# Other states of a selective scan take their forcing term through a diagonal matrix

## The reference, cut to what matters

```python
dt = softplus(proj[..., :512] + dt_bias)            # (T=256, 512 channels)
Bm, Cm = proj[..., 512:576], proj[..., 576:]        # (T, 64 states) each
A = -exp(A_log)
def step(hst, ins):
    dt_t, B_t, C_t, x_t = ins
    dA = exp(dt_t[:, :, None] * A)
    hst = hst * dA + (dt_t * x_t)[:, :, None] * B_t[:, None, :]
    y_t = einsum('bds,bs->bd', hst, C_t)
    return (hst, y_t)
```

## Time and profile before

| | |
|---|---|
| median of 3 runs | 3304.09 us (3300.77 to 3307.41) |
| the profiled execution | 3316.36 us, its span 3314.5 us |
| granted TensorE clock, mean | 0.97 of full speed |
| busy share of PE, PEld, DVE, ACT, POOL | 92%, 83%, 87%, 88%, 88% |
| the seventh pass (forward), 1350 to 1547 us | PE 189.7, DVE 181.9, ACT 180.7, POOL 181.4 us busy |
| the eighth pass (backward), 1547 to 1740 us | PE 180.2, DVE 176.5, ACT 181.2, POOL 182.6 us busy |

### The profile page before, as it was taken

How to read it: one execution, slowest core, us unless ns; L and a number is a source line. 1 busy time by engine, 2 the same in 40 slices (tenths; PEclk the granted TensorE clock), 3 DMA queues, 4 the chain that set the end, 5 groups by cost and what they waited for, 6 DMA issues and landing times.

```text
span 3314.5 us, 71769 instructions
## 1 busy us (share of the span) xinstructions
PE 3058.3 (92%) x23032; PEld 2760.6 (83%) x23032; DVE 2884.0 (87%) x3203; ACT 2904.8 (88%) x6357; POOL 2911.3 (88%) x1552
## 2 busy tenths in 40 slices
PE   8778999999999999999999999999999999998877
PEld 6568988898888988889888898888888898887766
DVE  2269999899989998899998999899988999989985
ACT  1189999898989989899998999899898989989993
POOL 0069999998999999999998999999999999999995
PEclk6699999999999999999999999999999999999998
DMA  5011111111111111111111111112111111111210
GB/s 179 0 42 45 45 46 54 43 52 44 46 51 45 52 44 47 51 50 44 46 54 44 51 45 45 53 45 52 44 47 50 51 46 45 45 50 44 55 47 26
DMA packets 163039, 162.61 MB, mean 49 GB/s; under 512 B 17610, under 2 KB 156874, under 8 KB 162644
## 3 DMA queue, kind: packets, MB, share of 16 engines
q1 hardware_dynamic: 162644, 157.69, 17.5%
HBM read 154.44 MB, written 3.18 MB: 48 GB/s over the span
## 4 chain that ended last, share of the span: by engine, by line
PE 50%; ACT 23%; issue 11%; DVE 8%; POOL 7%; DVEq 0%; ACTq 0%; POOLq 0%; DMA 0%; SPq 0%
PE ps L1263 13%; ACT dA L584 12%; PE ps L1247 12%; ACT uBT L570 6%; PE ps L1010 6%; POOL hst L417 5%; DVE hst L909 5%; PE ps L1245 4%; PE ps L1082 3%; PE ps L1019 3%; PE ps L1057 3%; PE ps L1066 1%; PE ps L1255 1%; PE ps L1131 1%; POOL uBT L430 1%
## 5 line engine op out<-in xcount | busy, mean ns | idle before, releaser
L417 POOL TENSOR_TENSOR hst<-hst,C_sb 128x1024 f32<-128x1024 f32 x1024 | 2447.3, 2407 | 176.1 <-DVE hst L909 172.7
L909 DVE TENSOR_TENSOR_SCAN hst<-dA,ps 128x512 f32<-128x512 f32 x2048 | 2376.7, 1203 | 146.3 <-PE ps L1263 112.9
L584 ACT ACTIVATE dA<-dt,A 128x255 f32<-128x255 f32 x4096 | 1745.0, 501 | 1.4 <-DVE hst L909 1.2
L1263 PE MATMUL ps<-ident,hst 128*128 128x128 f32 x8192 | 1240.7, 274 | 46.8 <-POOL hst L417 46.7
L1247 PE MATMUL ps<-ident,uBT 128*128 128x128 f32 x7104 | 1084.5, 275 | 52.6 <-DVE hst L909 39.8
L570 ACT ACTIVATE uBT<-uT,BT 128x512 f32<-128x512 f32 x1376 | 936.4, 717 | 117.3 <-PE ps L1247 89.2
L1263 PEld LDWEIGHTS ps<-ident,hst 128*128 128x128 f32 x8192 | 963.2, 141 | 62.9 <-POOL hst L417 62.2
L1247 PEld LDWEIGHTS ps<-ident,uBT 128*128 128x128 f32 x7104 | 844.6, 142 | 195.3 <-DVE hst L909 69.4
L430 POOL TENSOR_TENSOR uBT<-uT,BT 128x512 f32<-128x512 f32 x400 | 427.2, 1068 | 1.4 <-PE ps L1245 1.4
L1245 PE MATMUL ps<-uBT,uT 128*128 128x128 f32 x2176 | 302.7, 284 | 33.9 <-DVE hst L909 27.9
L1245 PEld LDWEIGHTS ps<-uBT,uT 128*128 128x128 f32 x2176 | 272.9, 197 | 45.7 <-DVE hst L909 35.9
(11 more groups left out here) (146 smaller groups left out, 2176.0 us busy)
## 6 DMA issues: line engine op xcount, KB each, us to landing
C_sb<-c_dram SPq DMA_DIRECT2D x1024, 128.0 KB, 2.9
gate_l<-gate_rows_dram SPq DMA_DIRECT2D x16, 256.0 KB, 3.8
x_att<-in_x_dram SPq DMA_DIRECT2D x8, 256.0 KB, 3.6
w<-in_L_cond_W_dram SPq DMA_DIRECT2D x2, 1024.0 KB
out_dram<-x_glu SPq DMA_DIRECT2D x8, 256.0 KB, 3.1
wg<-in_L_cond_mlp_w_dram SPq DMA_DIRECT2D x3, 512.0 KB, 11.0
w_xp<-_L_cond_fwd_xproj_w_dram SPq DMA_DIRECT2D x1, 1280.0 KB, 12.5
w_xp<-_L_cond_bwd_xproj_w_dram SPq DMA_DIRECT2D x1, 1280.0 KB, 14.4
```

The costliest lines, as they stand in the source:

```text
L417: pool.tensor_tensor(h, h, C_sb[:, n % FED:n % FED + 1, :].to_broadcast([P, KI, NB]), ALU.mult).then_inc(hC_ready.sem, 1)
L584: done = act.activation(dA[:, n % NT, c, lo:hi], dt[:, d, c, lo:hi], ACT.Exp, scale=A[:, d, c, n:n + 1])
L909: dve.tensor_tensor_scan(pair(hst[:, n % NR]), pair(dA[:, n % NT]), ps[:, BANK_U + (2 * n + e) % (2 * NU), :][:, way], 0.0, ALU.mult, ALU. ...
L1263: last = pe.matmul(ps[:, BANK_Y + j, c * P:(c + 1) * P], hst[:, n % NR, c, j * P:(j + 1) * P], ident[:, :], start=False, stop=(n == NS - 1 ...
```

## The change

One table is written anew. In the forward passes states 22 and 23 leave it and 28 and 29 enter, so that the run of six is 24 to 29 in place of 22 to 27; the number of states by diagonal stays ten. In the backward passes the even states 56 and 58 come in, and the run is 55 to 59.

```diff
-    BY_DIAGONAL = ((1, 3, 22, 23, 24, 25, 26, 27, 61, 63), (1, 3, 55, 57, 59, 61, 63))
+    BY_DIAGONAL = ((1, 3, 24, 25, 26, 27, 28, 29, 61, 63), (1, 3, 55, 56, 57, 58, 59, 61, 63))
```

## The result

The changed kernel takes **3333.77 us** (median of 6 runs, 3328.71 to 3337.68), the kernel before, run beside it, 3308.19 (3300.77 to 3310.09). The ratio is 1.0081, with a 95% interval of 1.0071 to 1.0091: 25.6 us slower, where the prediction had 5.2 and its range ended at +10.9. The profiled execution took 3336.83 us, with a span of 3335.0, 20.5 more than the one before, which was itself a slow one, 8.2 us over the 3308.19; so the traces have 20.5 us to place.

The account below looks back on a forecast made before the run. The prediction named no single bound: all four engines are busy 87 to 92%, and the end is decided stretch by stretch. Its terms, 5.9 - 0.3 - 0.4 = +5.2 us on the median 3304.09, gave 3309.3, range 3300 to 3315.

Parts of the forecast that it names:

- the "0 us" for the backward part: Backward passes, states 56 and 58: TensorE's 0.9 us more for each fits in its gaps, so 0 us.
- GpSimd ahead of L832, sized -0.3: Steady forward passes: GpSimd's L417 ends 0.42 us later, VectorE's L832 goes in right behind it; together -0.3 us.
- rival (a): Steady forward passes: L832 comes behind GpSimd's L427 again, giving 3312.7 us, slower; chance 0.22.
- The entry of "glu": Forward states 28 and 29: TensorE's added work delays VectorE's third L866 by 0.98 us a pass, 5.9 in six passes.
- the third L866: Steady forward pass, entry of "glu": VectorE waits 0.7 us more before this instruction, for TensorE's third product.
- the wait at L728: Steady forward pass: VectorE's wait for ScalarE's queue falls from 0.91 to 0.56 us.
- ScalarE's exact cover: Forward states 22 and 23: ScalarE's added 0.65 and 0.61 us exactly fill its 1.26 us idle before L516.
- The first pass: Whole pass: L832 0.8 us earlier, L835's meeting with GpSimd dealt anew; -3 to +2.3 us, taken as -0.4.
- the 15th pass, put at 0: TensorE-bound through states 22 to 30: 1.8 us goes and 1.8 comes, so 0.
- (b): Backward passes: TensorE bounds them too, 8 x 1.8 = 14.4 us more, giving 3324 us; chance 0.05.
- (c): Forward passes: the delay at the third L866 is absorbed before L728, leaving -0.7 us: 3303.4; chance 0.14.
- (d): Backward passes: ScalarE is the bound and its relief of 10.4 us counts, giving 3293.7 us; chance 0.09.

Follow-up runs that it names:

- experiment 2: Kernel before with only the backward list changed (56, 58 in): 3325.55 us, ratio 1.0042.
- experiment 3: Kernel before, lists untouched, with 32 empty instructions as TensorE's first: 3326.03 us, ratio 1.0046.
- experiment 1: Kernel before with only the forward list changed (22, 23 out, 28, 29 in): 3314.89 us, ratio 1.0024.
- experiment 5: Kernel before with 56 empty TensorE instructions ahead of everything: 3305.07 us, ratio 0.9997.
- experiment 6: Kernel before with 56 empty TensorE instructions and only the forward even state moved, 22 out, 28 in: 3311.28 us, ratio 1.0001.
- experiment 7: Kernel before with 56 empty TensorE instructions and only the forward odd state moved, 23 out, 29 in: 3313.03 us, ratio 1.0014.
- experiment 4: Changed kernel with 24 empty TensorE instructions ahead of everything: 3314.97 us, ratio to the kernel before 1.002.
- experiment 10: Changed kernel with TensorE's loop over the six middle blocks written out: 3313.04 us, ratio to the kernel before 1.0018.
- experiment 9: Kernel before with TensorE's loop over the six middle blocks written out, other engines keeping theirs: 3303.61 us, ratio 0.9982.
- experiment 8: Kernel before with 16 empty TensorE instructions ahead: 3310.98 us, ratio 1.0009.

## Why the prediction was wrong

It named 3309.3 us with 3300 to 3315 as the range, and most of the chance went to "the same". The time was 3333.8.

- **The step that failed is the "0 us" for the backward part.** The prediction goes through the change state by state and never asks what 32 more instructions ahead of a loop do to the code behind them. The work of states 56 and 58 did cost 0, in all eight passes; the instructions cost 14 us at five places where none of them executes: experiment 2 by its ratio 0.0042 x 3308 = 13.9, and states 0 to 4 behind the jumps 18.2 us with the second gap (after, experiments 2 and 3) against 15.4 without it (before, experiments 1, 5, 6 and 7), 5 x 2.8 = 14; with experiment 4's 13.8 among those without it, 15.1 and 15.5 us. Experiment 3 shows that the place alone does it, experiment 4 that it can be taken back with the change in place. The size is less sure than the cause: the medians say 17.2 and 17.7 for experiments 2 and 3, and 18.8 between the changed kernel and experiment 4.
- **GpSimd ahead of L832, sized -0.3, was rival (a).** L832 started 1.13 us before the L417's end, as worked out, but the L427 went first again in all six passes: +0.43 five times and +1.02 once, +3.2 in place of -0.3, against the +3.1 that was kept for the range. The evidence for it, five of the six meetings, was in the rows. I preferred the backward passes' behaviour, which was the wrong neighbour: there an L427 is running when L832 is asked for, and the L417 comes next. Experiment 7 ties it to state 23: in the five traces in which that state has left the diagonal (after, experiments 1, 4, 7 and 10) L832 takes 2.76 to 2.82 us in all 30 meetings. The -0.3 also took one execution's five to one as fixed, where seven traces have 28 to 14. By itself this miss would have stayed inside the range.
- **The entry of "glu" was right.** 0.98 a pass was forecast and 1.01 measured; the third L866 waits 0.64 (0.7 forecast), the wait at L728 falls to 0.60 (0.56). Of the 0.3 before the second L866, 0.24 came. Alone, the even state costs 0.1 there (experiment 6) and the odd one 0.6 (experiment 7), as the same working gives; the rest comes only with both.
- **ScalarE's exact cover held**: L516 has no idle time, and L524 comes no later.
- **The first pass** won 0.8 where -0.4 stood:

```profile
264.19 1.74 DVE L832 SCALAR_TENSOR_TENSOR qk<-uT,qk 128x1024 f32<-128x1024 f32 x1 [0.42 <-ACT uT L524]
...
269.20 2.95 DVE L835 TENSOR_TENSOR qk<-qk 128x1024 f32<-128x1024 f32 x1
```

  Counted from the first scan, L832 came 0.8 earlier, as worked out; it lasted 0.5 longer, and L835 met GpSimd 0.4 us shorter than in the earlier trace rows. The -0.4 was a guess within wide bounds, and so its miss says little. In the 15th pass, put at 0, 1.7 of the 2.1 us are the clock.
- **Rivals (b), (c) and (d)** did not happen. (b) had the number closest to the result, 3324, by a mechanism that is absent: no backward pass became bound by TensorE.

With the first two points and the first pass right, the forecast would have been 5.9 + 3.2 - 0.8 + 14 = +22, 3326 from the three runs that were shown. Those stood 4 us under the median of the six. Some 3 us of the 25.6 are not placed; they would be with the 17 us that the medians of experiments 2 and 3 give for the last term.

**What the gaps are, and what stays open.** Every packet of queue 8 moves 16,384 bytes, and the 46,064 matmuls and weight loads of experiment 9 in its 184 packets give 250 to a packet. In the ten traces with a loop, exactly one packet runs in each of the 50 gaps behind a jump: it starts 0.9 to 2.0 us behind TensorE's branch, and the first product follows 1.6 to 2.0 us behind its end. In each of the 19 second gaps one packet runs too, begun only 0.4 to 2.0 us behind that first product, and TensorE goes on 1.2 to 1.5 us behind its end. So TensorE's instructions come in such blocks, and the second gap is the wait for the block behind the one jumped into. In experiment 9 none of the 184 packets goes with a gap of the second kind. Where such a block begins was seen at one point only, and what decides the clock behind a gap was not tried further.

The Trainium skill (Runtime: NRT & Kernel Launch, "Instruction fetch mechanics") says that instructions come in blocks of 16 KiB, 256 instructions, that crossing a boundary costs "mostly hidden" time, and that a taken branch whose target is outside the window forces a fetch first. The block agrees with the packets' 16,384 bytes, the branch with the first gap of 2.5 to 3.7 us at every jump and with its absence in experiment 9. The boundary does not always: 18 instructions behind a jump it cost 1.2 to 3.0 us, 34 behind it 0.7 to 1.95 at four of five jumps.

## What to carry to other kernels

Where an engine has a loop, its instructions *ahead* of the loop decide where the loop's head falls in its instruction stream. Here 32 more of them cost about 14 us at five jumps without touching the work (TensorE's loop is the only one that was tried), so price the number of instructions as well as their time, and shift the head by some empty ones before judging an edit. Before trusting a cover, look at the passes' ends, not at a steady pass alone. And of two neighbours for an unknown meeting take the one in the same place of the program.

## What the runs showed of the hardware

- TensorE stands still for 2.5 to 3.7 us at each of the five jumps back (2.82 in the ninth pass before), while one packet of 16,384 bytes comes through queue 8; the profile names another engine as the releaser, or "issue". Writing the loop out takes that away: -5.2 us in all.
- A second standstill of 1.2 to 3.0 us follows when the jump's target lies 18 instructions ahead of a certain place of the stream (experiments 2 and 3), 0.7 to 1.95 us at 34 (experiment 8, four of five jumps), none that shows at 50 (before).
- Behind these gaps TensorE's granted clock often falls to half (at all five jumps before, at one of five in experiment 4): four sums take 1.06 us in place of 0.60. States 0 to 4 take 12.8 us at 1.00 and 14.4 at 0.88 with the same instructions (third and 15th passes), so one such fall costs 1.6 us of the whole kernel here, and it comes and goes from one execution to the next.
- VectorE's L832, asked for while GpSimd's L417 runs, came behind the *next* GpSimd instruction as well in all 30 meetings in which the L417 had 1.1 us left (2.8 us); with 0.7 us left it got in between in 14 of 42 (1.76).
